# Context attention and the last FFN of a two-layer decoder: mask, maxima, division and hidden product placed anew

## Reference

```python
def cross_attention(query, context, mask, Wq, bq, Wkv, bkv, Wout, bout, num_heads):   # 16 heads of 8
    ...
    scores = jnp.einsum('bhid,bhjd->bhij', q, k) * scale
    scores = jnp.where(mask[:, None, None, :], -jnp.inf, scores)
    attn = jax.nn.softmax(scores, axis=-1)
    out = jnp.einsum('bhij,bhjd->bhid', attn, v)
    ...
    return out @ Wout + bout

def fp4_quant_dequant(x):              # blocks of 16 along the last dim
    scale = jnp.maximum(jnp.max(jnp.abs(xb), axis=-1, keepdims=True) / 6.0, 1e-12)
    ...                                # each xb / scale to the nearest of 0, .5, 1, 1.5, 2, 3, 4, 6; times scale

gate = fp4_linear(x, w_gate); y = fp4_linear(x, w_up)      # 128 to 352, both operands quantized
h = jax.nn.silu(gate) * y
return fp4_linear(h, w_down)                               # 352 to 128, h quantized too
```

## Time and profile before

| what | value |
|---|---|
| median of 3 runs | 1257.46 us (1251.67 to 1261.6) |
| the profiled execution | 1253.11 us, span 1251.3 us |
| TensorE, VectorE, ScalarE, GpSimd busy | 90%, 72%, 70%, 50% of the span |
| granted TensorE clock, mean | 0.955 |
| chain that ended last | PE 33%, POOL 29%, issue 18%, DVE 16% |

### The profile page before, as it was taken

How to read it: one execution, slowest core, us unless ns; L and a number is a source line. 1 busy time by engine, 2 the same in 40 slices (tenths; PEclk the granted TensorE clock), 3 DMA queues, 4 the chain that set the end, 5 groups by cost and what they waited for, 6 DMA issues and landing times.

```text
span 1251.3 us, 17047 instructions
## 1 busy us (share of the span) xinstructions
...
## 2 busy tenths in 40 slices
...
DMA packets 25695, 14.48 MB, mean 12 GB/s; under 512 B 14622, under 2 KB 24460, under 8 KB 25484
## 3 DMA queue, kind: packets, MB, share of 16 engines
...
## 4 chain that ended last, share of the span: by engine, by line
PE 33%; POOL 29%; issue 18%; DVE 16%; ACT 2%; POOLq 0%; DMA 0%; SPq 0%; ACTq 0%; DVEq 0%
DVE ARENA L1170 6%; POOL ARENA L2730 6%; POOL ARENA L2728 5%; POOL ARENA L2724 5%; PE PS L1041 5%; POOL ARENA L2754 3%; POOL WQ L2741 3%; PE PS L911 3%; PE PS L1425 2%; PE PS L1015 2%; PE PS L1449 2%; PE PS L843 2%; PE PS L1416 2%; PE PS L859 2%; POOL WQ L2737 2%
## 5 line engine op out<-in xcount | busy, mean ns | idle before, releaser
L2580 DVE TENSOR_SCALAR ARENA<-PS,ARENA 128x512 f32<-128x512 f32 x256 | 171.9, 742 | 51.9 <-PE PS L2217 51.5
L1170 DVE TENSOR_REDUCE ARENA<-PS 128x1 f32<-128x512 f32 x256 | 160.7, 682 | 27.6 <-PE PS L859 26.9
L1086 ACT ACTIVATE ARENA<-PS 128x1024 f32<-128x1024 f32 x128 | 128.7, 1025 | 60.3 <-PE PS L897 60.0
L2398 ACT ACTIVATE ARENA<-ARENA 128x2048 f32<-128x2048 f32 x64 | 121.9, 1911 | 51.6 <-DVE ARENA L2580 51.0
L2217 PE MATMUL PS<-ARENA 64*128 64x512 f32 x512 | 139.7, 644 | 0.0
L2405 ACT ACTIVATE ARENA<-ARENA,consts_sb 128x2048 f32<-128x2048 f32 x64 | 124.7, 1995 | 0.4
L2227 PE MATMUL PS<-ARENA 128*64 128x512 f32 x512 | 119.3, 609 | 1.5 <-issue 1.5
L2411 ACT ACTIVATE ARENA<-ARENA 128x2048 f32<-128x2048 f32 x64 | 118.4, 1899 | 0.0
L1351 POOL TENSOR_TENSOR ARENA<-ARENA 128x512 f32<-128x512 f32 x32 | 40.7, 1270 | 119.8 <-DVE ARENA L1309 119.3
L2737 POOL TENSOR_SCALAR WQ<-ARENA,consts_sb 128x512 bf16<-128x512 f32 x32 | 22.2, 692 | 146.5 <-DVE ARENA L2556 146.5
L859 PE MATMUL PS<-ARENA 32*128 32x512 bf16 x256 | 71.9, 404 | 26.1 <-DVE ARENA L1170 20.7
...
## 6 DMA issues: line engine op xcount, KB each, us to landing
...
```

What stands on the lines that cost most here:

```text
L1086: act.activation(PT[m % PT_SLOTS], bank(("cP", m)), ACT.Exp, scale=0.5).then_inc(sem("c_exp"), 1)
L1170: dve.tensor_reduce(NMX[:, w % 2, t, h:h + 1], bank(("cS", n, j)), AX.X, ALU.max, negate=True).then_inc(sem("c_max"), 1)
L2398: act.activation(chunk(u, half), chunk(u, half), ACT.Sqrt).then_inc(sem("rooted"), 1)
L2580: dve.tensor_scalar(D[:, u % 2, kt, hd, :], bank(("S", u, c)), K2[:, u % 2, kt, hd:hd + 1], 1e-30, ALU.add, ALU.max).then_inc(sem("guarded ...
```

## The change

In context attention TensorE adds the mask with a bf16 identity product on top of the scores, in the same bank. VectorE takes the maxima out of PSUM and subtracts them while it moves the scores to SBUF; the scale goes into ScalarE's exponential. GpSimd has no step in a tile any more. The exponentials are transposed undivided, one step earlier; the values' products have 32 columns of weights for each 32 output partitions, four more such products with a matrix of ones by head give the sums (`eZ`), ScalarE inverts these by logarithm and exponential (`invert_sums`), and VectorE multiplies once per batch (`weighted`). The constant `vhead` shrinks from 512 to 32 columns, and GpSimd spreads the values in one instruction, not four. The mask's preparation has three more small instructions, for rows without a valid position (`MNAN`).

In the FFN the product of SiLU and up goes back into the up banks, and block maxima and scaling read it there; the down product lands in the free quarter of the banks of `fT`. Gate and up of a step are made two steps ahead, in pools of their own. Batch 2's activation is quantized in hidden step 1, batch 3's still in step 2. In the last step VectorE does GpSimd's two passes itself, and the step's halves go separately through transpose, copy, down product and add. The residual adds of batches 2 and 3 come behind the first hidden step.

```diff
-    vmask = np.zeros((P, 4, P))
-    for g in range(4):
-        vmask[:, g, :] = (part[None, :] // DX == (4 * g + head)[:, None])
-    cols["vhead"] = vmask.reshape(P, -1)
+    cols["vhead"] = (part[:, None] // CK == np.arange(4 * DX)[None, :] // DX).astype(np.float32)
...
+    def values(b, pool):
+        return [(("eO", b), 1, [("e_o", b + 1)], pool), (("eZ", b), 1, [("e_sum", b + 1)], pool)]
+
+    def project_out(b, pool):
+        return [(("eX", b), 1, [("x_new", 4 * B + b + 1)], pool)]
...
+        if s >= 1:
+            b, t = divmod(s - 1, QT)
+            jobs += [(("eT", s - 1), 1, [("e_pt", s)], pool_at(s))]
             if t == 1 and b:
-                jobs += [(("eX", b - 1), 1, [("x_new", 4 * B + b)], pool_at(s))]
-            if t == 0 and b >= 2:
-                jobs += [(("fX", b - 2), 1, [("f_x", b - 1)], pool_at(s))]
-    jobs += [job + ("E4",) for job in gate_and_up_jobs(0)]
-    return jobs + [(("eO", B - 1), 1, [("e_o", B)], "E2"), (("eX", B - 1), 1, [("x_new", 5 * B)], "E2"),
-                   (("fX", B - 2), 1, [("f_x", B - 1)], "E2")]
+                jobs += values(b - 1, pool_at(s))
+            if t == 1 and b >= 2:
+                jobs += project_out(b - 2, pool_at(s))
+            if s == FIRST_QUANTIZED:
+                jobs += [(("fX", 0), 1, [("f_x", 1)], pool_at(s))]
+    jobs += values(B - 1, "E2") + gate_and_up_jobs(0) + project_out(B - 2, "E01") + project_out(B - 1, "E01")
+    return jobs + [(("fX", 1), 1, [("f_x", 2)], "fG")]
+
+
+FIRST_QUANTIZED = 15
...
+            jobs += [(("fT", n), 2, [("f_ht", n + 1), ("x_final", n + 1)], "fT")]
+        else:
+            jobs += [(("fL", j), 1, [("f_ht", last + 1 + j)], "fG") for j in range(2)]
...
-            link(dve.tensor_copy(MB[:].rearrange("p b j -> p (b j)"), MK8[:]))
-            dve.tensor_scalar(MB[:], MB[:], -3e38, 10.0, ALU.mult, ALU.mult).then_inc(sem("mask_bias"), 1)
+            link(dve.tensor_copy(MF[:].rearrange("p b j -> p (b j)"), MK8[:]))
+            dve.tensor_scalar(MB[:], MF[:], -1e30, None, ALU.mult).then_inc(sem("mask_bias"), 1)
+            link(dve.tensor_reduce(MNAN[:, 0], MF, AX.X, ALU.min))
+            link(dve.tensor_scalar(MNAN[:, 0], MNAN[:, 0], -3e38, 10.0, ALU.mult, ALU.mult))
+            dve.tensor_tensor(MNAN[:, 1], MNAN[:, 0], MNAN[:, 0], ALU.subtract).then_inc(sem("mask_nan"), 1)
...
-                done(pe.matmul(o, QTX[:, b, t * P:(t + 1) * P], KX[:, b].rearrange("p h j -> p (h j)"), start=True, stop=True),
-                     ("eS", n))
+                pe.matmul(o, QTX[:, b, t * P:(t + 1) * P], KX[:, b].rearrange("p h j -> p (h j)"), start=True, stop=False)
+                pe.wait_ge(sem("mask_bias"), 1)
+                done(pe.matmul(o.rearrange("p (h j) -> p h j", h=HX), identb[:], MB[:, b].unsqueeze(1).to_broadcast([P, HX, CK]),
+                               start=False, stop=True), ("eS", n))
...
-                    mm = pe.matmul(o, VX[b][:, g, :], PTE[:, b % 2, g, :], start=g == 0, stop=g == 3)
+                    r = slice(32 * g, 32 * g + 32)
+                    mm = pe.matmul(o[r, :], VX[:, b, r], PTE[:, b % 2, g, :], start=True, stop=True)
                 done(mm, ("eO", b))
+                o = begin(("eZ", b))
+                for g in range(4):
+                    r = slice(32 * g, 32 * g + 32)
+                    mm = pe.matmul(o[r, :], const("vhead"), PTE[:, b % 2, g, :], start=True, stop=True)
+                done(mm, ("eZ", b))
...
-            for s in range(STEPS + 2):
+            for s in range(STEPS + 1):
                 d_tail(s)
                 for n in scores_at(s):
                     scores(n)
-                if s < 2:
+                if s < 1:
                     continue
-                n = s - 2
+                n = s - 1
                 b, t = divmod(n, QT)
-                pe.wait_ge(sem("e_p"), n + 1)
+                pe.wait_ge(sem("e_exp"), n + 1)
                 o = begin(("eT", n))
-                p = SE[n % 7].rearrange("p h j -> p (h j)")
+                p = SE[n % 6].rearrange("p h j -> p (h j)")
                 for g in range(4):
                     mm = pe.transpose(o[:, g * P:(g + 1) * P], p[:, g * P:(g + 1) * P], ident)
                 done(mm, ("eT", n))
-                if t == 0 and b:
+                if t == 1 and b:
                     values(b - 1)
-                if t == 1 and b:
-                    project_out(b - 1)
-                if t == 0 and b >= 2:
-                    turn_quantized(b - 2)
+                if t == 1 and b >= 2:
+                    project_out(b - 2)
+                if s == FIRST_QUANTIZED:
+                    turn_quantized(pe, begin, done, 0)
+            values(B - 1)
             pe.wait_ge(sem("f_w"), 3)
             gate_and_up(pe, begin, done, 0)
-            values(B - 1)
+            project_out(B - 2)
             project_out(B - 1)
-            turn_quantized(B - 2)
+            turn_quantized(pe, begin, done, 1)
...
+            def invert_sums(b):
+                full(act, ("eZ", b))
+                if b:
+                    act.wait_ge(sem("e_o"), b)
+                act.activation(ISUM, bank(("eZ", b)), ACT.Ln).then_inc(sem("e_sum"), 1)
+                act.wait_ge(sem("e_sum"), b + 1)
+                act.activation(ISUM, ISUM, ACT.Exp, scale=-1.0).then_inc(sem("e_isum"), 1)
+
+            for n in range(STEPS + 2):
                 b, t = divmod(n, QT)
                 d_tail(n)
-                if t == 1 and b >= 2:
-                    rstd(5, b - 2)
                 if n < STEPS:
                     act.wait_ge(sem("e_shift"), n + 1)
-                    act.activation(SE[n % 7], SE[n % 7], ACT.Exp).then_inc(sem("e_exp"), 1)
-                if n == STEPS + 2:
-                    silu(act, 0)
-                if n >= 3:
-                    turned(n - 3)
-                if t == 3 and 1 <= b < B:
-                    out_copy(b - 1)
-                if t == 3 and b >= 2:
-                    quantized_out(act, b - 2)
-            out_copy(B - 1)
-            quantized_out(act, B - 2)
+                    act.activation(SE[n % 6], SE[n % 6], ACT.Exp, scale=SCALEX).then_inc(sem("e_exp"), 1)
+                if n >= 2:
+                    turned(n - 2)
+                if t == 3 and b:
+                    invert_sums(b - 1)
+                if t == 2 and b >= 2:
+                    rstd(5, b - 2)
+                if n == FIRST_QUANTIZED + 1:
+                    quantized_out(act, 0)
+            invert_sums(B - 1)
+            silu(act, 0)
...
-                dve.scalar_tensor_tensor(out=SE[n % 7], in0=bank(("eS", n)).rearrange("p (h j) -> p h j", h=HX),
-                                         scalar=SCALEX, in1=MB[:, b].unsqueeze(1).to_broadcast([P, HX, CK]),
-                                         op0=ALU.mult, op1=ALU.add).then_inc(sem("e_biased"), 1)
-                dve.wait_ge(sem("e_biased"), n + 1)
-                dve.tensor_reduce(NME[:, n % 2], SE[n % 7], AX.X, ALU.max).then_inc(sem("e_max"), 1)
-
-            def sums(n):
-                dve.wait_ge(sem("e_exp"), n + 1)
-                if n >= 3:
-                    dve.wait_ge(sem("e_p"), n - 2)
-                link(dve.tensor_reduce(SUE[:, n % 3], SE[n % 7], AX.X, ALU.add))
-                dve.reciprocal(RCE[:, n % 3], SUE[:, n % 3]).then_inc(sem("e_rc"), 1)
-
-            for n in range(STEPS + 2):
+                dve.tensor_reduce(NME[:, n % 2], p, AX.X, ALU.max).then_inc(sem("e_max"), 1)
+                if n >= 6:
+                    full(dve, ("eT", n - 6))
+                dve.wait_ge(sem("e_max"), n + 1)
+                dve.tensor_tensor(SE[n % 6], p, NME[:, n % 2].unsqueeze(2).to_broadcast([P, HX, CK]), ALU.subtract
+                                  ).then_inc(sem("e_shift"), 1)
+
+            def weighted(b):
+                full(dve, ("eO", b))
+                dve.wait_ge(sem("e_isum"), b + 1)
+                if b >= 2:
+                    full(dve, ("eX", b - 2))
+                dve.wait_ge(sem("mask_nan"), 1)
+                dve.scalar_tensor_tensor(out=OTE[:, b % 2], in0=ISUM, scalar=MNAN[:, 1, b:b + 1], in1=bank(("eO", b)),
+                                         op0=ALU.add, op1=ALU.mult).then_inc(sem("e_o"), 1)
+
+            def add(b):
+                dve.wait_ge(sem("xb4"), b + 1)
+                add_to_stream(4, b, ("eX", b))
+                stats(5, b)
+
+            for n in range(STEPS):
                 b, t = divmod(n, QT)
-                if n < STEPS:
-                    shift(n)
-                if n >= 2:
-                    sums(n - 2)
+                shift(n)
                 d_tail(n)
-                if b >= 2 and t == 0:
-                    dve.wait_ge(sem("xb4"), b - 1)
-                    add_to_stream(4, b - 2, ("eX", b - 2))
-                    stats(5, b - 2)
-                if b >= 2 and t == 1:
-                    normalize(5, b - 2)
-                if b >= 2 and t == 2:
```

(110 more changed lines are left out.)

171 lines of the change are left out of this document (75 added, 96 removed).

## The result

The changed kernel takes 1238.85 us (median of 4 runs, 1234.58 to 1242.39) against 1258.31 (median of 4, 1251.67 to 1261.6): a ratio of 0.9856, with a 95% interval of 0.9809 to 0.9904. Faster, by 0.96 to 1.9%. A second round of both gave 1239.59 against 1254.82, 0.9881 (0.9844 to 0.9918). The forecast was 1246, in a range of 1233 to 1258: 11.5 us less than its 1257.46, where the two rounds of medians measured 19.5 and 15.2 less. The profiled execution took 1234.58 with a span of 1232.8.

The account below looks back on a forecast made before the run. Bound: TensorE's end of window attention until 1119.30, then VectorE with some waits until 1239.43, then a serial tail. Terms 0 - 8.2 - 1.8 - 3.3 + 2 - 0.3 = -11.6 us, from 1257.46 to 1246; range 1233 to 1258.

Parts of the forecast that it names:

- 1088 to 1119.3: First piece of context attention, ended by TensorE's window attention work: no gain, 0, bounds -1 and +2 us.
- 1119.3 to 1182.26: Rest of context attention up to the second FFN: 63.0 us becomes 54.8, a gain of 8.2.
- The clock's 5: Within 1119.3 to 1182.26: 5 us added for TensorE products at half clock: values 1, projection 0, scores 12, projection 1, values 3.
- The 6.5: Within 1119.3 to 1182.26: VectorE's waits at full clock: first context output, scores 12, root 1, inverse sums 2, SiLU 0.
- 1182.26 to 1239.43: Second FFN's hidden steps: 57.2 us becomes 55.4, gain 1.8, as PSUM operands avoid waits behind GpSimd.
- Rival 3: Hidden steps: product in PSUM doesn't free VectorE from GpSimd, six steps wait 1.3 us more each; -4, 1253.5; chance 0.08.
- The tail: After the last quantizing step, 9.1 us: VectorE rounds itself and halves overlap, 5.8; gain 3.3 (2.3 to 4).
- Masks: Mask preparation in window attention: a minimum and two tiny instructions that may wait for GpSimd passes, +2 us (0 to 2.4).
- Start: Kernel start: constants 256 KB smaller, so ScalarE waits less for them; gain 0.3 us (0 to 0.5).
- rival 1: Everything drains at full clock and mask instructions fall between GpSimd's passes: -20, 1237.5 us; chance 0.2.
- Rival 2: ScalarE's in-order queue behind the roots: both batches lose 4 us more; -3.6, 1254 us; chance 0.12.
- Rival 4: Many short waits hold TensorE at half clock from 1119 on: +10, 1267 us; chance 0.1.

Follow-up runs that it names:

- e8: Changed kernel without TensorE's product that adds the mask, so scores are unmasked; the mask is still prepared: 1241.54 us, 0.9889 of before.
- e5: Changed kernel with the variance roots of batches 0 and 1 computed one tile later on ScalarE: 1236.3 us, 0.9853 of before.
- e1: Changed kernel with the hidden product and its block maxima back in SBUF instead of PSUM: 1247.39 us, 0.9938 of before.
- e4: Changed kernel plus unused TensorE products filling idle time behind the last turned tiles, hidden steps 5 and 6 and the next to last down product: 1236.2 us.
- e9: Changed kernel with e5's later roots and the three instructions for rows with nothing to attend to moved into the attention, no added products: 1230.32 us.
- e10: Changed kernel plus three unused TensorE products in its wait behind the masks: 1237.15 us, 0.9854 of before.

## Why the prediction was right, and where its terms were off

The side and the range held, the size was underrated: -18.5 us between the profiled spans, -15.2 from Z on, for a forecast of -11.6.

- **1088 to 1119.3, "nothing":** -1.1. The bank held twice shows at two tiles, not three, and TensorE waits 0.91 and 0.30 us for it, where I had said about 1 each; the mask product costs 1.2 here (e8), which I had put beside other work. Both were more than given back. The shorter values are 1.7 of it by the rows above (3.53 us from the start of batch 0's values to the next instruction before, 1.86 now); that the rest is the earlier turning is argued.
- **1119.3 to 1182.26, forecast -8.2:** -12.2. The 43.3 us of work were right: 50.76 less 8.4 of waits is 42.4. By the views of both pieces VectorE's busy time went from 54.9 us to 40.5, its idle time from 8.1 to 10.3 (short gaps between instructions included), so the gain is VectorE's work and not its waits. The waits were mis-sized: 8.4 for "6.5 + 5". The clock's 5 was the wrong term: values 1 took 1.06 and 1.04 us, full clock, where the earlier trace rows had shown 0.55; half clock came mainly at the last score tile (1.92 us) and values 3, and the waits leave 1.9 for it. The 6.5 were right one by one: 1.91 us for the 2.0 at the first context output, 2.58 for the 2.5 at score tile 12 behind ScalarE's root, which e5 shows as the cause, and 0.60 and 1.09 for the 1.6 at root 1 and inverse sums 2. The 4.6 us that e5 finds for the two roots are about what those 2.5 and 1.6 had for them.
- **1182.26 to 1239.43, forecast -1.8:** -3.5. Steps measured 5.84 for 5.80, normalizations 1.11 for the 1.48 taken from the earlier trace rows, quantizing 5.03 for 5.3, one wait of 1.02 for the 1.5 of slow stretches. e1 shows the mechanism, PSUM operands run free beside GpSimd, and its price of 5.4. The Trainium skill, "SBUF — State Buffer", section "SBUF: two separate sides", has a VectorE operation with two SBUF inputs, or in a two-port mode, wait for the whole of a GpSimd instruction that began before it: the trace agrees, 1.29 us ending with GpSimd against 0.20. Rival 3 is out.
- **The tail, forecast -3.3:** -2.2, and 6.9 us from the last rounding add to the last residual add, where under 6 was to be the sign. The step that failed is the path: I let the halves flow, but TensorE's queue had the down product of step 6 in front of them, at half clock. At full clock (e4, e9) that product ends as the first half is ready (in e9 at 1225.5), and the tail gains 4.5, more than forecast. The clock term belonged here.
- **Masks, forecast +2:** two small instructions each waited for one GpSimd pass, as said, 2.0 us with the minimum. What I left out is what follows: a product of VectorE behind them can meet a further pass, TensorE waits for VectorE there, and in six of the seven variants that keep the masks in place it came back at half clock, +2.9. A-B is +1.5 in the changed kernel's own executions and +5.7 in those six (+2.8 in e10, which fills the wait); 2.4 more, which only the changed kernel has, lie ahead of the masks, unexplained.
- **Start, -0.3:** the constants got 240 KB smaller (465 to 225), not 256, and ScalarE's first root came 0.47 earlier (5.24 for 5.71). Whether the end gained by it can't be seen in the 3 us by which executions of one kernel differ before Z.

**Rivals.** The total, 1238.85, came next to rival 1's 1237.5, which is luck, for it came by another way: the granted clock from C to D was fuller, 0.93 where the kernel before has 0.81, but the masks cost more, not nothing. Rival 2 was right in place and wrong in size: the two roots did hold the queue, 4.6 us, but the forecast had that already, and the 8 us more that the rival put on top didn't come. Rival 4, half clock throughout, did not come: 0.92 over 1088 to 1182. The larger fixed time of a PSUM source, which I had left out ("VectorE: DVE Perf Modes", section "The TRN2 errata", in the Trainium skill), doesn't show in these passes either: 0.68 us for maxima out of PSUM, 0.69 out of SBUF.
